# GpSimd's 704-element operations of the FP4 quantisation in two pieces of 352

## The reference

```
def fp4_quant_dequant(x):
    xb = x.reshape(shape[:-1] + (shape[-1] // BLOCK, BLOCK))
    scale = jnp.max(jnp.abs(xb), axis=-1, keepdims=True) / 6.0
    scale = jnp.maximum(scale, jnp.float32(1e-12))
    xn = xb / scale
    idx = jnp.searchsorted(_MID, jnp.abs(xn))
    q = _GRID[idx] * jnp.sign(xn) * scale
...
gate = fp4_linear(x, w_gate)
y = fp4_linear(x, w_up)
h = jax.nn.silu(gate) * y
return fp4_linear(h, w_down)
```

## Time and profile before

| what | us |
| --- | --- |
| median of 3 runs | 2169.54 |
| lowest and highest | 2167.63, 2172.38 |
| the profiled execution | 2175.12 |
| its span, first to last instruction | 2173.3 |
| busy: PE, DVE | 1791.2, 1366.8 |
| busy: GpSimd, ACT | 961.6, 803.1 |

### The profile page before, as it was taken

The page is one execution under the profiler, slowest core; times in us unless marked ns, Lnnn a source line. Parts: engine busy times, 40 slices in busy tenths (PEclk is TensorE's granted clock), DMA queues, the critical chain, the costliest instruction groups (busy, mean ns, idle before and its releaser), DMA issues.

```text
span 2173.3 us, 51626 instructions
## 1 busy us (share of the span) xinstructions
PE 1791.2 (82%) x21261; PEld 1259.5 (58%) x21261; DVE 1366.8 (63%) x2749; ACT 803.1 (37%) x1298; POOL 961.6 (44%) x1266
## 2 busy tenths in 40 slices
PE   2899999999999998878999987777776777777774
PEld 2566666666666666655555556666665455555553
DVE  5744445555455553565555555678777688888875
ACT  0233333333333332324444443333433444444442
POOL 1522223333322323443434345589886455555533
PEclk7999999999999999989999999879888788888987
DMA  4000000000000000023333323233332222232210
GB/s 159 1 2 1 1 2 1 1 1 1 1 1 1 2 1 1 16 59 74 70 78 71 77 60 74 46 83 82 79 85 60 59 55 57 64 64 64 58 27 8
DMA packets 167464, 89.54 MB, mean 41 GB/s; under 512 B 9393, under 2 KB 165810, under 8 KB 166978
## 3 DMA queue, kind: packets, MB, share of 16 engines
q1 hardware_dynamic: 167010, 85.70, 17.1%
q0 software_dynamic: 224, 0.54, 0.1%
HBM read 46.36 MB, written 39.85 MB: 40 GB/s over the span
## 4 chain that ended last, share of the span: by engine, by line
PE 48%; DVE 35%; issue 6%; ACT 5%; POOL 2%; DVEq 0%; DMA 0%; POOLq 0%; SPq 0%; ACTq 0%
PE slots L1302 34%; DVE nmx L1194 13%; PE ctx_ps L1302 9%; DVE rope_part L1235 6%; DVE rope_part L1159 2%; PE slots L1577 2%; ACT ctxT L1000 1%; DVE band_r L1160 1%; DVE band_va L626 1%; DVE ctxT L1278 1%; DVE band_va L629 1%; ACT probs L1080 1%; DVE rope_part L1160 1%; ACT band_va L1000 1%; DVE band_va L624 1%
## 5 line engine op out<-in xcount | busy, mean ns | idle before, releaser
L1194 DVE TENSOR_REDUCE nmx<-slots 128x8 f32<-128x1024 f32 (+2 forms) x352 | 407.9, 1216 | 107.9 <-PE slots L1302 104.7
L1080 ACT ACTIVATE probs<-slots 128x1024 f32<-128x1024 f32 (+1 forms) x416 | 356.0, 892 | 302.4 <-PE slots L1302 299.2
L1302 PE MATMUL slots<-band_r 64*64 64x64 bf16 (+4 forms) x5120 | 392.4, 262 | 85.3 <-DVE nmx L1194 42.4
L1302 PEld LDWEIGHTS slots<-band_r 64*128 64x128 bf16 (+2 forms) x5120 | 192.9, 120 | 254.9 <-issue 126.9
L1235 DVE SCALAR_TENSOR_TENSOR rope_part<-slots,bias_qk,rope_band 128x256 f32<-128x256 f32 x512 | 212.3, 477 | 197.4 <-PE slots L1302 173.3
L1302 PE MATMUL ctx_ps<-probs,band_va 64*32 64x64 f32 (+4 forms) x5120 | 257.0, 312 | 47.6 <-issue 24.5
L979 POOL TENSOR_TENSOR band_r<-rope_part 128x512 f32<-128x512 f32 x128 | 164.3, 1284 | 251.0 <-DVE rope_part L1235 251.0
L1302 PE MATMUL slots<-mask,ident_bf 128*128 128x256 bf16 (+1 forms) x896 | 217.0, 324 | 45.9 <-DVE nmx L1194 16.5
L1302 PEld LDWEIGHTS ctx_ps<-probs,band_va 128*32 128x32 f32 (+2 forms) x5120 | 145.4, 118 | 129.8 <-issue 66.0
L893 POOL TENSOR_TENSOR var_eps<-mean_var,eps 128x2 f32<-128x2 f32 x128 | 29.2, 228 | 430.4 <-DVE mean_var L1122 430.4
L1302 PE MATMUL slots<-nmT,pick 64*128 64x256 bf16 (+2 forms) x2560 | 217.6, 240 | 1.5 <-issue 1.4
(11 more groups left out here) (173 smaller groups left out, 2926.9 us busy)
## 6 DMA issues: line engine op xcount, KB each, us to landing
band_r<-scratch SPq DMA_DIRECT2D x192, 192.0 KB, 4.4
scratch<-parts SPq DMA_DIRECT2D x96, 192.0 KB, 2.2
scratch<-parts SPq DMA_DIRECT2D x96, 128.0 KB, 2.1
scratch<-parts SPq DMA_DIRECT2D x96, 64.0 KB, 1.9
x<-in_x SPq DMA_DIRECT2D x16, 128.0 KB, 2.8
out<-x SPq DMA_DIRECT2D x16, 128.0 KB, 1.8
band_r<-in_band_qk_a SPq DMA_DIRECT2D x1, 1024.0 KB, 6.3
band_r<-in_band_qk_b SPq DMA_DIRECT2D x1, 1024.0 KB, 7.9
```

The source lines that it names most:

```text
L1080: nc.scalar.activation(probs[:, g % 2, step[2], :, 0:width], slot(u, step).rearrange("p (a n) -> p a n", a=2)[:, :, 0:width], ACT.Exp, sca ...
L1194: nc.vector.tensor_reduce(dst, src, axis=AX.X, op=ALU.max, negate=True).then_inc(free_sem(u, step), 1)
L1302: return nc.tensor.matmul(o, lhsT, rhs, start=start, stop=stop, skip_group_check=shared)
```

## The change

`quantise` gets an argument `pieces`, 1 unless given. Operations 6, 7 and 8 are emitted once for each piece of the columns, a whole number of blocks in each; every one but the last of the series is linked. Only GpSimd's call for the hidden products passes 2, so each of its three operations of 704 elements becomes two of 352, in the order 6, 6, 7, 7, 8, 8, all linked. The other calls emit what they did. The planner's times and the engines' orders are as before.

```diff
-        def quantise(v, link, buffers, dst, src, n, keep, which):
+        def quantise(v, link, buffers, dst, src, n, keep, which, pieces=1):
...
-                lambda: v.tensor_tensor(qx, qx, qp, ALU.add),
-                lambda: v.tensor_tensor(qx, qx, qp, ALU.subtract),
-                lambda: v.tensor_tensor(by_block(dst), by_block(qx), spread(amax), ALU.mult))
+                lambda at, blocks: v.tensor_tensor(qx[:, at], qx[:, at], qp[:, at], ALU.add),
+                lambda at, blocks: v.tensor_tensor(qx[:, at], qx[:, at], qp[:, at], ALU.subtract),
+                lambda at, blocks: v.tensor_tensor(by_block(dst[:, at]), by_block(qx[:, at]),
+                                                   amax[:, blocks].unsqueeze(2).to_broadcast([P, blocks.stop - blocks.start, BLOCK]), ALU.mult))
             for i in which:
-                last = ops[i]()
-                if i < len(ops) - 1:
+                if i < 6:
+                    last = ops[i]()
                     link(last)
+                    continue
+                for k in range(pieces):
+                    part = slice(k * blocks // pieces, (k + 1) * blocks // pieces)
+                    last = ops[i](slice(part.start * BLOCK, part.stop * BLOCK), part)
+                    if i < len(ops) - 1 or k < pieces - 1:
+                        link(last)
             return last
...
                         quantise(nc.gpsimd, link, hidden_q, hq.rearrange("p t c -> p (t c)"), None, TILES * HID1, 0.5,
-                                 QUANT_OPS[2]).then_inc(hq_ready, 1)
+                                 QUANT_OPS[2], 2).then_inc(hq_ready, 1)
```

## The result

The changed kernel took 2160.15 us (median of 5 runs, 2157.60 to 2163.22) beside 2170.29 for the kernel before in the same comparison: 10.1 us faster, a ratio of 0.9953 with a 95% interval of 0.9938 to 0.9967 (7.2 to 13.5 us). The forecast was 2156.0 and -13.5 us; the time lies inside the range of 2147 to 2165, the gain at the small end of what was expected. The profiled execution took 2163.22 us with a span of 2161.4.

The account below looks back on a forecast made before the run. DVE, held by GpSimd's long operations, was taken to bound the lowrank attention units; -16.0 there, +2.2 in the drain and +0.3 in the chunk stage gave -13.5 us, so 2156.0 us from 2169.54, range 2147 to 2165.

Parts of the forecast that it names:

- DVE's instructions get in at a piece's end: Lowrank units: DVE's held token instructions enter at GpSimd piece boundaries, so the tokens are done 1.29 to 1.98 us sooner.
- the case that L630 comes too late: Lowrank units: GpSimd's fourth piece starts before DVE's L630 gets in, which then ends at 4.16 us instead of 3.47.
- The duration of a piece: GpSimd's operations of 352 elements should take 0.93 and 0.79 us, from a line through 256 and 704 elements.
- Rival (d): A piece costs nearly what 512 elements do, 1.29 us; no gain in the units, about 2171 us; 5%.
- The gain per unit, 1.14 us: Lowrank units: of DVE's saving, 1.14 us gets through, as PE's L1366 starts at 1793.43 instead of 1794.57.
- Sum of the 14 units, 16.0 us: The 14 lowrank units with DVE on the chain gain 14 x 1.14 = 16.0 us.
- The drain, +2.2: From 2100 us GpSimd's longer series is on the chain three times: 3 x 0.75 = +2.2 us.
- The chunk stage, +0.3: Sixteen chunk units: gaps cover GpSimd's added 0.72 us except where tight units meet; +0.3 us, bounds 0 and 11.5.
- Rival (b): GpSimd bounds the chunk stage, about ten tight units paying 0.72 us in full: +7 us, 2163 us; 13%.
- (a): All of DVE's saving gets through in the lowrank units: 14 x 1.98 = 27.7, less 2.5, giving 2144 us; 7%.
- (c): DVE doesn't get in between pieces of one operation, so each unit is 0.72 us longer: +12.6, 2182 us; 4%.

Follow-up runs that it names:

- the clock kept up: Addition and subtraction in two pieces in the 14 middle units, lowrank score fills computed twice, against the kernel before: 2146.93 us, ratio 0.9887.

## Why the prediction was right, and where a term was off

- **DVE's instructions get in at a piece's end.** Right. L624 and L626 came out at 0.42 and 0.94 us, and the tokens at 4.18 us after the series' start; the working had 4.16 for the case that L630 comes too late. It always came too late (0.99 us, with 0.09 to 0.10 us behind the piece's start). That splitting the first operation alone gives nothing followed from the same working.
- **The duration of a piece.** Right: 0.932 and 0.948 us for 0.93, and 0.786 for 0.79. The straight line through 256 and 704 elements held. Rival (d) is out.
- **The gain per unit, 1.14 us.** The mis-sized term. PE was found in the right place as the next to bound, but its slack was read from one unit: 0.48 us before L1343 and 0.69 before L1366, with a product with V of 1.23 us. In the other regular units of the same trace the first wait is anything from 0 to 0.68 us, as that product takes 1.80 to 1.07. In the changed kernel it settles at 1.93, 0.70 more than in the unit read, both waits are gone, and the regular distance fell by 0.55 us. With the clock kept up it fell by 1.17. That lies beside the predicted 1.14 by chance: the 1.14 was PE's slack, and in that kernel it is DVE that bounds.
- **Sum of the 14 units, 16.0 us.** 14.4 in the trace. It came closer than the regular distance allows, since the distances of 29.02 and 30.95 us, which I had only averaged in, fell by 1.7 to 3.5: with the waits for the maxima went a low stretch of the clock that I hadn't looked at. The mean of the first 13 distances fell from 28.4 to 27.4, where 27.3 was forecast. That the sum came out near 16.0 was in part luck.
- **The drain, +2.2.** Each series is 0.8 us longer, 2.4 in all, as worked out. The profiled execution shows +3.9; the 1.5 above that is also there in five kernels with nothing changed in the drain (1.3 to 1.7).
- **The chunk stage, +0.3.** Nothing to be seen above the spread of 293 to 303 us between kernels whose quantisation is the same there. Rival (b), +7, is out by the kernel with the pieces outside the middle: +7 and the drain's 2.4 would be 9.4 us, and its interval ends at 2.8.
- **Rivals (a) and (c).** (a), all of DVE's saving, is out for this kernel: five microseconds less work on DVE gave 27.3 us as well. With the clock kept up nearly all of it did get through. (c), DVE passed over at the boundaries, is out in every trace. GpSimd waited for DVE only a little, as on the row read: the subtraction's pieces take 948 ns on average and the addition's 932. The exclusive lock that the Trainium skill states (SBUF — State Buffer, "two separate sides") agrees with DVE's side beside these long operations in all of these kernels.

The forecast of -13.5 us is at the edge of the interval of the changed kernel (-7.2 to -13.5). The kernel with the pieces in the middle alone measured -13.7; the number to set beside it is the -16.0 of the prediction's 14 units, since it has none of the drain's cost.

**A better version.** Pieces where DVE stands beside them and nowhere else, the multiplication whole, and PE's lowrank score fills computed twice: 2146.93 us, 24.4 less than the kernel before, with the same values computed.

## What to carry to other kernels

An engine with slack can still be the cause of a busy one's length: compare the durations of one and the same instruction alone and beside a GpSimd operation, and see whether they end together. Before splitting, work out for each held instruction which piece it meets next, since freeing the first few can be worth nothing, and where the second chain stands. And read that second chain in several units, with its clock: the slack of 0.48 us in one unit was 0 to 0.68 in others, because TensorE's low stretch didn't move with the units. Keeping PE busy paid about 10 us once DVE was freed and nothing before. A unit that is longer than its neighbours is worth a look at the clock before it is averaged in.

## What the runs showed of the hardware

One more kernel had GpSimd's three operations on the products replaced by three linked memsets of 1380 elements; the rounding and last scaling of the products are left out.

```diff
+                        link(nc.gpsimd.memset(pad[:], 0.0))
+                        link(nc.gpsimd.memset(pad[:], 0.0))
+                        nc.gpsimd.memset(pad[:], 0.0).then_inc(hq_ready, 1)
```

> The kernel before with GpSimd's three operations on the hidden products left out and three linked memsets of 1380 elements (about 1.27 us each, they write SBUF and read nothing) in their place; the rounding and the final scaling of the products are left out. If GpSimd holds every DVE instruction that needs the second pair of ports, L624, L626 and L629 are held until a memset ends, as before. If only instructions in the two-port mode need what a write holds, the tensor_scalars (L624, L629, L630) are held and L626, with two SBUF inputs, takes its 0.42 us.

It took 2153.68 us in its only run, too few to compare; twelve of its distances are 27.27 to 27.32 us. GpSimd and DVE (its `quantise` is one line lower in the file, so L624 is L625):

```profile
1832.68 1.25 POOL L971 MEMSET pad<- 128x1380 f32 x1 [2.92 <-DVEq L1172]
1833.99 1.25 POOL L972 MEMSET pad<- 128x1380 f32 x1
1835.29 1.27 POOL L973 MEMSET pad<- 128x1380 f32 x1
```

```profile
1833.24 0.72 DVE L625 TENSOR_SCALAR band_va<-band_va 128x16 f32<-128x16 f32 x1
...
1834.28 0.43 DVE L627 TENSOR_TENSOR band_va<-band_va 128x256 f32<-128x256 f32 x1
1834.74 0.64 DVE L630 TENSOR_SCALAR band_va<-band_va 128x256 int32<-128x256 int32 x1
1835.42 1.30 DVE L631 TENSOR_SCALAR band_va<-band_va 128x256 f32<-128x256 f32 x1
```

Beside a GpSimd operation that only writes, the multiplication with two SBUF inputs takes its 0.43 us; beside GpSimd's L632, which reads SBUF, it was held (1.69). The tensor_scalars are held by both. The Trainium skill (SBUF — State Buffer, "Who interferes with whom") says that an instruction with two SBUF inputs contends with GpSimd's reads only and a two-port one with either; the trace agrees on both in these rows. It doesn't agree everywhere. In the kernel before, GpSimd's L915, which reads the tokens from SBUF, runs beside the same multiplication eleven times in the chunk stage, and each time the multiplication takes its free 0.42 us, as here:

```profile
1413.23 0.79 POOL L915 TENSOR_SCALAR xn<-x,mean_var,rstd 128x128 f32<-128x128 f32 x1
...
1413.60 0.42 DVE L626 TENSOR_TENSOR band_va<-band_va 128x256 f32<-128x256 f32 x1
```

Why this one doesn't hold it is open.

And at a boundary of 0.08 us between two linked GpSimd operations a waiting DVE instruction got in every time in the 14 units of these traces, while L630, issued 0.09 to 0.10 us behind the start of the next, was too late every time.
